# One megakernel of graph attention and a mixture of experts: a residual sum moved to TensorE, the order of ranks and slots changed, fills left out, weights loaded by expert, six buffers of weighed rows

## The reference

```python
def gnn(h, adj, W, a):
    Wh = h @ W
    e = Wh @ a[:D] + swapaxes(Wh @ a[D:], 1, 2)
    e = where(e > 0, e, 0.2 * e)
    e = where(adj > 0, e, -inf)
    return elu(softmax(e, -1) @ Wh)

def ffn(x, Wg, bg, W1, b1, W2, b2):          # 8 experts, hidden 512, top 2
    scores, idx = top_k(x @ Wg.T + bg, 2)
    p = softmax(scores)
    # combine[e] = p of expert e where it is one of the two, else 0
    out = sum over e of combine[e] * (relu(x @ W1[e].T + b1[e]) @ W2[e].T + b2[e])
    return out

x = x + gnn(layernorm(x), adj, W, a)
x = x + ffn(layernorm(x), Wg, bg, W1, b1, W2, b2)
```

## Time and profile before

| | before |
|---|---|
| median of three runs | 440.06 us |
| profiled execution | 442.13 us, its span 440.3 us |
| PE busy | 407.3 us (93%) |
| PEld busy | 308.3 us (70%) |
| DVE busy | 358.9 us (82%) |
| ACT busy | 321.3 us (73%) |
| POOL busy | 289.0 us (66%) |
| granted TensorE clock, mean | 0.991 of full speed |
| stages | graph 0 to about 163 us, drain to about 190, experts to about 417, end sums to 440 |

### The profile page before, as it was taken

How to read it: one execution, slowest core, us unless ns; L and a number is a source line. 1 busy time by engine, 2 the same in 40 slices (tenths; PEclk the granted TensorE clock), 3 DMA queues, 4 the chain that set the end, 5 groups by cost and what they waited for, 6 DMA issues and landing times.

```text
span 440.3 us, 9161 instructions
## 1 busy us (share of the span) xinstructions
PE 407.3 (93%) x2272; PEld 308.3 (70%) x2290; DVE 358.9 (82%) x1410; ACT 321.3 (73%) x760; POOL 289.0 (66%) x292
## 2 busy tenths in 40 slices
PE   7998999889998888999999999999999999999980
PEld 3656666666666665688878888888888888876630
DVE  5689999999998898999887887777778778757683
ACT  2678887888888987688888678778767877866500
POOL 1041777777777777777777777767667657764662
PEclk9999999999999999999999999999999999999996
DMA  5995334333333344443632433322233233297888
GB/s 181 293 390 193 102 115 118 108 103 104 100 101 104 97 128 122 128 133 98 200 99 95 122 102 101 115 90 84 91 90 90 66 84 90 79 289 247 248 310 316
DMA packets 44004, 63.04 MB, mean 143 GB/s; under 512 B 7744, under 2 KB 24512, under 8 KB 43712
## 3 DMA queue, kind: packets, MB, share of 16 engines
q1 hardware_dynamic: 30448, 34.88, 26.5%
q0 software_dynamic: 9344, 20.10, 13.6%
q10 hardware_dynamic: 4176, 7.66, 5.3%
HBM read 27.28 MB, written 26.94 MB: 123 GB/s over the span
## 4 chain that ended last, share of the span: by engine, by line
PE 63%; DVE 20%; ACT 5%; DMA 5%; issue 4%; SPq 1%; POOL 1%; DVEq 0%; ACTq 0%; POOLq 0%
PE bank L1441 7%; PE bank L1455 7%; PE bank L1454 7%; PE bank L1457 7%; PE bank L1445 7%; PE bank L1442 7%; PE bank L1425 3%; PE bank L1433 3%; PE bank L1403 3%; PE bank L1316 3%; DVE xn L1066 3%; PE bank L1401 3%; DVE bn L901 2%; DVE neg_max L1048 2%; DVE score L1043 2%
## 5 line engine op out<-in xcount | busy, mean ns | idle before, releaser
L520 POOL DMA_INDIRECT expert_slots<-rows,slot_i x128 | 126.4, 987 | 55.4 <-issue 33.5
L712 ACT ACTIVATE yb<-bank,b_sb 128x512 f32<-128x512 f32 x36 | 24.8, 688 | 51.8 <-PE bank L1457 51.8
L1454 PE MATMUL bank<-hh,w_hi 128*128 128x512 f32 x144 | 60.1, 417 | 0.0
L1441 PE MATMUL bank<-xh,w_hi 128*128 128x512 f32 x144 | 58.5, 406 | 0.9 <-ACT xh L697 0.5
L1455 PE MATMUL bank<-hh,w_lo 128*128 128x512 f32 x144 | 57.4, 398 | 0.0
L1445 PE MATMUL bank<-xl,w_hi 128*128 128x512 f32 x144 | 56.9, 395 | 0.2 <-DVE xl L1122 0.2
L1457 PE MATMUL bank<-hl,w_hi 128*128 128x512 f32 x144 | 56.8, 395 | 0.3 <-DVE hl L1153 0.3
L1442 PE MATMUL bank<-xh,w_lo 128*128 128x512 f32 x144 | 56.8, 395 | 0.0
L536 POOL DMA_INDIRECT moe_rows<-hrelu,ysi x40 | 41.2, 1030 | 17.6 <-issue 10.7
L536 POOL DMA_INDIRECT moe_rows<-hexp,ysi x40 | 40.9, 1023 | 17.7 <-issue 10.1
L1146 DVE CAST hh<-z 128x512 fp32r<-128x512 f32 x36 | 16.5, 459 | 42.3 <-ACT z L702 41.9
(11 more groups left out here) (166 smaller groups left out, 1051.0 us busy)
## 6 DMA issues: line engine op xcount, KB each, us to landing
rows<-xn SPq DMA_DIRECT2D x32, 256.0 KB
xs<-expert_slots SPq DMA_DIRECT2D x27, 260.0 KB
x_all<-x SPq DMA_DIRECT2D x16, 256.0 KB, 3.5
w_raw<-w_t SPq DMA_DIRECT2D x2, 2048.0 KB, 13.7
w_raw<-moe_rows SPq DMA_DIRECT2D x16, 256.0 KB, 4.5
out<-x_all ACTq DMA_DIRECT2D x16, 256.0 KB, 4.7
xs<-expert_slots ACTq DMA_DIRECT2D x11, 260.0 KB
w_hi<-moe_rows SPq DMA_DIRECT2D x9, 256.0 KB, 4.1
```

Source lines behind the costliest of these rows:

```text
L520: nc.gpsimd.indirect_dma_start(out=slots, out_offset=bass.IndirectOffsetOnAxis(ap=slot_i[q][:, k * SUB + j:k * SUB + j + 1], axis=0), in_= ...
L712: nc.scalar.activation(yb[:, :], ps_y[:, :], ACT.Identity, bias=b2_sb[:, e:e + 1]).then_inc(yb_ok, 1)
L1441: nc.tensor.matmul(ps_h[c][:, :], w1_hi[:, e, chunk], xh[:, :], start=True, stop=False)
L1454: nc.tensor.matmul(ps_y[:, :], w2_hi[:, e, c, :], hh[:, c, :], start=c == 0, stop=False)
```

## The change

TensorE now adds x, relu(h) and -1 into the attention's PSUM bank (`elu_plus`: two float32 products with the identity and one bf16 product of the identity with a constant -1), and VectorE adds min(exp(h), 1) from there in one operation (`residual_plus`) where it had two (`elu_sum`, `residual`). In TensorE's step the rank comes behind z from step 5 on, `elu_plus` and the turns of the second norm come ahead of Wh, and the fills ahead of the turns are gone except in steps 1 and 2. In VectorE's step the slots come behind the maximum from step 6 on; the copy of the indices to float32, one addition of epsilon and three semaphore increments are gone. ScalarE takes the first of four softmax exponentials at the end of the step before, and the copy of Wh between the exponentials and the turned softmax. SyncE loads the experts' weights one expert at a time between the passes of groups 0 to 7. There are six buffers of weighed rows (the two new ones are `xn2`), a third pad tile, and VectorE's turns are written out where they were loops. The drain keeps the old two operations.

```diff
-BUFS = 4
-QUADS = 7
+BUFS = 6
+LAPS = 4
+MORE = 4
+FIXED = BUFS * LAPS + MORE
-FILL_STEP, FILL_NORM = 3, 8
-FILL_EARLY, EARLY = 9, (1, 2)
+FILL_STEP = 3
+EARLY = {1: 9, 2: 1}
+RANK_LAST = 5
...
-        ys = [hrelu, hexp, u, xn1]
+        ys = [hrelu, hexp, u, xn1] + xn2
...
-            sp.dma_start(w1_raw[:, :, :], w1_t).then_inc(c_w1, 16)
-            sp.dma_start(w2_raw[:, :, :, :], w2_t).then_inc(c_w2, 16)
...
+            for g in range(SURE_GROUPS + 1):
+                pass_on(g // 2, g % 2)
+                if g < E:
+                    sp.dma_start(w1_raw[:, g, :], w1_t[:, g, :]).then_inc(c_w1, 16)
+                    sp.dma_start(w2_raw[:, g, :, :], w2_t[:, g, :, :]).then_inc(c_w2, 16)
...
-                    softmax_exp(g1)
+                    softmax_exp(g1, range(1, SUB))
...
+                    copy_wh(g1)
                     turned_prob(g1)
...
+                if isinstance(t, int) and t + 1 < len(BATCHES):
+                    first_root(t + 1)
                 if g0 is not None:
-                    act.wait_ge(wh_ps, g0 + 1)
-                    nc.scalar.copy(wh[:, :, :], tiles(ps_wh)).then_inc(wh_ok, 1)
+                    softmax_exp(g0, range(1))
...
+            def residual_plus(gx):
+
+                dve.wait_ge(hexp_ok, gx + 1)
+                dve.wait_ge(plus_ps, gx + 1)
+                nc.vector.scalar_tensor_tensor(x_all[:, bass.ds(gx, 1), :, :].rearrange("p g s d -> p (g s) d"),
+                                               hexp[:, :, :], 1.0, tiles(ps_av), ALU.min, ALU.add).then_inc(x2_ok, 1)
...
                 dve.wait_ge(x2_ok, gx + 1)
-                dve.sem_inc(met, 1)
...
-                last = nc.vector.tensor_scalar(var2[:, 0, :], mv2[:, :, 1], EPS, None, ALU.add)
+                n = norms(gx)
+                nc.vector.tensor_scalar(var2[:, 0:n, :], mv2[:, 0:n, :, 1], EPS, None, ALU.add).then_inc(var2_ok, 1)
...
-                nc.vector.tensor_copy(top_f[:, :, :], top_i[:, :, 0:2].rearrange("p t k -> p k t")).then_inc(topf_ok, 1)
-                dve.wait_ge(topf_ok, gl + 1)
...
+            def elu_plus(g1):
+
+                pe.wait_ge(hrelu_ok, g1 + 1)
+                pe.wait_ge(hexp_ok, g1 + 1)
+                if not later(g1):
+                    pe.wait_ge(ones_ok, 2)
+                nc.tensor.matmul(ps_av[:, :], ident, x_all[:, g1, :, :].rearrange("p s d -> p (s d)"), start=True, stop=False)
+                nc.tensor.matmul(ps_av[:, :], ident, hrelu[:, :, :].rearrange("p s d -> p (s d)"), start=False, stop=False)
+                nc.tensor.matmul(ps_av[:, :], ident_b[:, :], minus_b[:, None, :].to_broadcast([P, SUB, P]), start=False, stop=True
+                                 ).then_inc(plus_ps, 1)
```

## The result

The change makes the kernel faster, by 0.5%, which is clear of the noise but less than forecast. Median 438.92 us (436.54 to 440.46) against 440.65 of the kernel before on the same chips (439.52 to 442.1), 21 executions each; ratio 0.995, 95% interval 0.9939 to 0.9962, so 2.2 us where 5.75 were forecast. The profiled execution took 440.12 (span 438.3), 2.0 less than before.

A forecast was written before the change was run, and what follows sets the result against it. The graph stage's step loop (10.16 us) bounds, then GpSimd's scatters (10.15 a group). Slack of 4.4 in the drain plus GpSimd's 1.35 gives 5.75: 440.06 - 5.75 = 434.3 us, range 429.5 to 438.5.

The forecast's parts named there:

- the loop: Graph stage, score to score: with the rank behind z a step takes 9.05 us in place of 10.16.
- GpSimd's start: Scatters of group 2 start at 61.1, 1.35 us earlier, from step 6's score at 59.0 plus 2.1 for the slots.
- What is late next: By step 10 VectorE's L1008 waits for scatters, steps take 10.15 again; VectorE gains 4.4 + 1.35 = 5.75 us at group 14.
- The drain: Behind the graph stage: the 5.75 us gained at the scatter wait carry to the first weighed rows, 186.0 for 191.75.
- elu_plus: TensorE's added products in a graph-stage step: 1.9 us in all, at most 2.55.
- the second norm's turns: TensorE in a graph-stage step: they come about 1.7 us after the score.
- the turned softmax: Graph-stage step: lands about 5.1 us after the score, hidden by 0.4 behind the roots, which wait until 5.5.
- scatters 1.26 apart: GpSimd in the graph stage: scatters stay 1.27 us apart throughout, 10.15 a group, which the change does not shorten.
- weights, buffers and catching up: Expert stage: weight loading, six buffers and GpSimd starting 4.4 us further behind VectorE are hidden and cost nothing.
- B: Rival, graph stage: dear `elu_plus` and late turned softmax keep steps at 9.9, gain 2 to 3 us, 437.6; chance 0.18.
- C: Rival, TensorE: the fills kept its clock; without them steps at half clock make it slower, 448 us; chance 0.07.
- D: Rival, graph stage: L1008 or late slots cost GpSimd what the loop wins; time stays at 440 us; chance 0.04.

The follow-up runs named there:

- the run with the reciprocal early: Changed kernel with VectorE's reciprocal `inv_sum` moved ahead of the choice of experts; ratio 0.9943 to the kernel before.
- the run with fills in the drain: Changed kernel with eight fill products between the second and third product of the drain's first hidden block; ratio 0.9927 to the kernel before.
- three buffers alone: Changed kernel with three buffers of rows for the scatters in place of two, reciprocal not moved; ratio 0.9904 to the kernel before.
- low halves later: Changed kernel with rank ahead of z in every step and the second expert's low weight halves moved behind the drain's block table; ratio 1.0027 to the kernel before.
- the fastest form: Changed kernel with `inv_sum` ahead of the choice of experts and three buffers of rows for the scatters; median 431.94 us against 441.04, ratio 0.9793.
- four buffers: The fastest form with four buffers of weighed rows in place of six; ratio 0.9911 to the kernel before.
- the rank ahead: The fastest form with the rank ahead of z and the slots ahead of the score in every step; ratio 0.9872 to the kernel before.
- the two with the fills back: Elu's sum and residual on VectorE, eleven fills a step back on TensorE: in the changed kernel 0.9944, in the fastest form 0.9880, to the kernel before.

## Why the prediction was wrong

The sign was right, the size not: 434.3 forecast, 438.92 measured, outside the range by 0.4. Two steps of the prediction failed, the loop and GpSimd's start; the run with the reciprocal early mended the first and gained nothing, so the lost microseconds go by the second and by what followed from it. By its own steps:

- *The loop* failed. Each term of it was measured within 0.1, and 9.05 is what a step takes when the loop is the one I summed. What I left out is a second path: `inv_sum` waits behind `choose` on VectorE, the elu on ScalarE for `inv_sum`, and the copy of z stands behind the elu. Before the change it was hidden, because the rank held z back longer, but only just: the earlier trace rows show ScalarE idle for 0.25 ahead of the copy of z, and the elu is what it had done until then. Moving the rank shortened the one path by 1.1, and the step by 0.27. The row of the kernel before that stands at the head of the second path, 6.86 behind the score (6.96 after):

```profile
98.59 0.17 DVE L1080 RECIPROCAL inv_sum<-psum_row 128x4 f32<-128x4 f32 x1
```

- *GpSimd, its start*, failed too: 61.1 forecast, 63.06 measured. The score of step 6 is at 60.20 and not at 59.0 (1.2 late): up to the score of step 5 (50.55) 0.54 was gained where 1.1 was forecast, and step 5, already at the longer loop, gained 0.5 where 1.1 was forecast. And from the end of the slots (62.22) to the first scatter it is 0.84, which I had not priced (0.84 too with the early reciprocal). GpSimd's first send of results is at 209.97, 1.0 later than before, where 207.6 was forecast.
- *What is late next*: VectorE waits for scatters, as said, but the gain there is 2.3 and not 5.75. GpSimd ends group 11 0.76 later than before, not 1.35 earlier (2.1), and its landing took 2.9 and not the 1.6 of the earlier trace rows (1.3): 5.75 - 2.1 - 1.3 = 2.35. What delayed this one landing is open; that of the next group took 1.4. With GpSimd the cap, the failed loop costs the end only through GpSimd's start.
- *The drain* gave back 0.8, where I took the gain to carry over one for one: the 2.3 at the weights of group 13 are 1.6 at those of group 14 (179.62 against 181.21 in the earlier trace rows), behind the wait of 1.58 for the gate. The products ahead of the gate at the low clock cost 1.0 of that wait by the run with fills in the drain; that the 0.8 are the clock's alone is argued, not shown.
- *Right*: elu_plus at 2.0 (1.9 forecast), the second norm's turns 1.65 behind the score, the turned softmax 5.1 behind it, scatters 1.26 apart, weights, buffers and catching up at nothing (GpSimd waits for VectorE in 19 sends, as the waits of the changed kernel have it in total, times and longest; forecast were 16).

```profile
POOL moe_rows L530 <- DVE ysi L1148: 24.9, 19, 2.4
```

- *Rivals.* B has the number, 9.9 a step and 2 to 3 us, but not the mechanism: neither elu_plus nor the turned softmax is late. C has a mechanism that exists: the fills did hold the clock, and elu_plus now does, but less well: besides the drain, six kept traces with elu_plus lose it in a step between scores 13 and 16 (the early reciprocal, fills in the drain, three buffers alone, low halves later, and in the fastest form four buffers and the rank ahead), while the two with the fills back lose it in no step from 3 on. D comes near for GpSimd: the slots behind the maximum cost it what the first steps had won.

Open: which executions lose the clock, and where. The windows show it in one stretch in some and another in others, with the same program up to there; the executions of the changed kernel spread over 3.9 us, those of the kernel before over 2.6. Of the 21 executions of the changed kernel the four with a mean clock of 0.991 or 0.992 have a median of 437.4, the 17 others (0.985 to 0.989) of 439.4; the profiled one (0.988) is among the 17.

## What to carry to other kernels

When an edit shortens a loop through several in-order engines, sum not only the path that was longest: for each operation on it, look at what stands ahead of it on its own engine and at that one's releasers, since the second path was hidden only by the first. Where another engine runs back to back beside the loop, ask when its first item starts and how many buffers lie between, for shorter steps become waits there. And products whose result nobody reads may be what keeps TensorE's clock, as here: undo them alone.

## What the runs showed of the hardware

- A scatter's landing is not a fixed time behind the row's end. In the changed kernel it took 1.4 us for group 10 (154.21 to SyncE's pass at 155.61) and for group 12 (175.52 to 176.92), but 2.9 for group 11 (164.81 to 167.70); 1.4 for group 11 with the early reciprocal (163.48 + 0.97 to 165.84), 1.6 for group 4 before. The Trainium skill (Perfetto Trace Analysis, DMA Instruction — SWDGE (GPSIMD)) says only that the end of the row is not the landing; these runs agree, and show the spread.
- GpSimd's indirect scatters follow each other at 1.26 us in the graph stage (0.96 and 0.30 of issue), before the change as after it. The first scatter of group 2, which had to wait for its slots, started 0.84 behind the VectorE operation that wrote its slots (62.22 to 63.06; 61.33 to 62.17 with the early reciprocal).
